# y from high and low parts of x and of the condition's weights, in three fp32r passes from the ninth tile on

## The reference

```python
W = cond_weights[condition]                      # (64, 64, 64)
y = einsum('bct,bcd->bdt', x, W)                 # (64, 64, 1024)
base = einsum('bsi,oi->bso', y, W_org)
q = einsum('bi,ki->bk', y.mean(axis=1), Wq)
coeffs = softmax(einsum('bk,ek->be', q, lora_keys) / sqrt(128))
h = einsum('bsi,eir->bser', y, lora_down)        # 8 experts, rank 64
delta = einsum('be,bser,ero->bso', coeffs, h, lora_up)
out = x + base + delta
```

## Time and profile before

| | |
|---|---|
| median of 3 runs | 714.96 us (714.73 to 715.47) |
| profiled execution | 714.7 us, span 712.9 us |
| PE busy | 701.1 us (98%) |
| PE weight loads | 587.1 us (82%), beside the matmuls |
| DVE busy | 505.9 us (71%) |
| ACT busy | 286.5 us (40%) |
| POOL busy | 118.2 us (17%) |
| instructions | 10677 |

### The profile page before, as it was taken

How to read it: one execution, slowest core, us unless ns; L and a number is a source line. 1 busy time by engine, 2 the same in 40 slices (tenths; PEclk the granted TensorE clock), 3 DMA queues, 4 the chain that set the end, 5 groups by cost and what they waited for, 6 DMA issues and landing times.

```text
span 712.9 us, 10677 instructions
## 1 busy us (share of the span) xinstructions
PE 701.1 (98%) x3345; PEld 587.1 (82%) x3345; DVE 505.9 (71%) x821; ACT 286.5 (40%) x580; POOL 118.2 (17%) x108
## 2 busy tenths in 40 slices
PE   8999999999999999999999999999999999999997
PEld 7877787888888888888888878888888888888876
DVE  3888687585784864655656997786777677776774
ACT  4456665856666742443524822221122222211220
POOL 2210000000000000000000033323332333333360
PEclk9999999999999999999999999999999999999999
DMA  8987376484684754423443846666676776766732
GB/s 240 280 260 232 106 231 209 145 255 149 192 244 149 207 194 128 137 104 90 135 160 121 316 136 194 221 214 219 219 235 237 236 236 220 233 203 213 268 119 88
DMA packets 100986, 138.60 MB, mean 194 GB/s; under 512 B 18874, under 2 KB 70082, under 8 KB 98114
## 3 DMA queue, kind: packets, MB, share of 16 engines
q1 hardware_dynamic: 100592, 137.85, 60.0%
q10 hardware_dynamic: 338, 0.07, 0.0%
HBM read 82.32 MB, written 55.57 MB: 193 GB/s over the span
## 4 chain that ended last, share of the span: by engine, by line
PE 87%; DVE 6%; issue 4%; DMA 1%; SPq 1%; ACT 1%; POOL 0%; DVEq 0%; ACTq 0%; POOLq 0%
PE x_ps L1456 23%; PE w_ps L1456 17%; PE x_ps L1378 11%; PE h_ps L1378 11%; PE x_ps L1412 11%; PE w_ps L1412 8%; PE y_ps L1337 6%; DVE tb_l L873 1%; DVE tu_l L873 1%; DVE blk L876 1%; DMA t_dram<-st 1%; DVE up_raw L873 1%; DVE ysum L889 1%; DMA cw_sb<-in_L_cond_weights_dram 0%; DVE ba_l L873 0%
## 5 line engine op out<-in xcount | busy, mean ns | idle before, releaser
L566 POOL TENSOR_TENSOR blk<-blk,blkx 128x512 f32<-128x512 f32 x60 | 93.1, 1552 | 276.3 <-DMA blkx<-in_x_dram 160.4
L876 DVE TENSOR_TENSOR blk<-w_ps,blk 128x512 f32<-128x512 f32 x96 | 66.1, 688 | 68.1 <-PE w_ps L1412 32.4
L1456 PE MATMUL x_ps<-tb_h,ba_h 128*128 128x512 f32 x256 | 100.0, 390 | 0.8 <-DVE ba_l L873 0.4
L1456 PE MATMUL x_ps<-tb_l,ba_h 128*128 128x512 f32 x256 | 99.6, 389 | 0.0
L1456 PE MATMUL x_ps<-tb_h,ba_l 128*128 128x512 f32 x256 | 99.6, 389 | 0.0
L602 ACT ACTIVATE ba_h<-bs 128x512 fp32r<-128x512 f32 x64 | 38.1, 626 | 125.7 <-DVE bs L873 125.7
L1456 PE MATMUL w_ps<-tb_h,ba_h 128*128 128x512 f32 x192 | 74.9, 390 | 0.0
L1456 PE MATMUL w_ps<-tb_h,ba_l 128*128 128x512 f32 x192 | 74.7, 389 | 0.0
L1456 PE MATMUL w_ps<-tb_l,ba_h 128*128 128x512 f32 x192 | 74.7, 389 | 0.0
L602 ACT ACTIVATE ba_h<-yb 128x512 fp32r<-128x512 f32 x48 | 28.4, 621 | 101.9 <-DMA yb<-y_dram 101.9
L876 DVE TENSOR_TENSOR blk<-x_ps,blk 128x512 f32<-128x512 f32 x64 | 42.5, 683 | 34.2 <-PE x_ps L1456 34.2
(11 more groups left out here) (100 smaller groups left out, 1407.8 us busy)
## 6 DMA issues: line engine op xcount, KB each, us to landing
x_sb<-in_x_dram SPq DMA_DIRECT2D x32, 512.0 KB, 4.3
y_dram<-y_full SPq DMA_DIRECT2D x64, 256.0 KB, 3.1
yb<-y_dram SPq DMA_DIRECT2D x32, 512.0 KB, 7.3
out_dram<-blk SPq DMA_DIRECT2D x64, 256.0 KB, 3.9
blkx<-in_x_dram SPq DMA_DIRECT2D x30, 512.0 KB, 6.8
r_dram<-blk SPq DMA_DIRECT2D x56, 256.0 KB, 2.5
blk<-r_dram SPq DMA_DIRECT2D x14, 1024.0 KB, 6.7
t_dram<-st SPq DMA_DIRECT2D x16, 448.0 KB, 4.3
```

The source lines that it names most:

```text
L566: pool.tensor_tensor(blk[p % 3][:, b, :], blk[p % 3][:, b, :], blkx[:, h, n, :], ALU.add).then_inc(x_added, 1)
L876: nc.vector.tensor_tensor(dst, a, b, ALU.add).then_inc(done, 1)
L1456: mm = nc.tensor.matmul(bank, ba[s][n][:, k, :], tb[w][n][:, k, :], start=(first and k == 0 and i == 0), stop=(k == 3 and i == 2), skip_gr ...
```

## The change

From tile 8 on (TS = 8), y is made of parts. The two buffers of x for tile t are: raw and then, in place, the low part in buffer t % 2; the high part in buffer 2 + t % 2, both as `x_hl`, an fp32r view of the same memory as `x_sb`. So there are two buffers of raw x in place of four, and `load_x(t)` waits for the tile two back. ACT's `split_x(t)` copies x to its high part (128x1024, fp32r), DVE's subtracts it. POOL makes two instructions of each tile's weights: the high part `cwh` (in the memory of cws) and the low part `cwl`. PE makes three matmuls of 128 columns per product: high x high, high x low, low x high.

Each loop q splits the third and fourth tile of its own y (4q+6, 4q+7) amid the h blocks, in loops 1 to 6, and the first two of the next loop's (4q+8, 4q+9) amid the up products, in loops 0 to 5. To make room, `yg` moves into the memory of `gs`, with waits in `gate_sums` for whoever reads gs; two semaphores are folded into others.

```diff
@@ -90,6 +90,8 @@
         yq = [at(f"yq_{s}", 90112 + 16384 * n, [P, KC, N], F32R) for n, s in enumerate("hl")]
         y_full = at("y_full", 122880, [P, 8, 4, P])
         x_sb = at("x_sb", 139264, [P, 4, IN])
+        x_hl = at("x_hl", 139264, [P, 4, IN], F32R)
         g32 = at("g32", 155648, [P, 2, EC, 2 * P])
         ga = [at(f"ga_{s}", 163840 + 7168 * n, [P, NS, 2, P], F32R) for n, s in enumerate("hl")]
         gs = at("gs", 178176, [P, 4, 2, P])
...
@@ -131,13 +133,17 @@
         cw_sb = small("cw_sb", [P, 4, BT, C])
         cws = small("cws", [P, 3, BT, 2, C // 2])
+        cwh = at("cwh", spot[0] - 12 * P, [P, 3, BT, 2, C // 2], F32R)
+        cwl = small("cwl", [P, 3, BT, 2, C // 2], F32R)
         ident = small("ident", [P, P])
         ones_r = small("ones_r", [P, P], F32R)
         gate = small("gate", [P, E, KC])
         keys_sb = small("keys_sb", [E, K])
         keys_t = small("keys_t", [K, E])
         ysum = small("ysum", [P, KC, BQ])
-        yg = small("yg", [P, BQ, E, KC])
+        yg = at("yg", 178176, [P, BQ, E, KC])
         z = small("z", [P, BQ * E])
         zs = small("zs", [P, 2, BQ * E], F32R)
         ssb = small("ssb", [P, BQ, E])
...
@@ -284,6 +291,24 @@
         def tile_made(t):
             return max(made(2 * t), made(2 * t + 1))
+        TS = 8
+        def x_at(t):
+            return t % 4 if t < TS else t % 2
+        def x_count(t):
+            return 16 * (t // 4 + 1 if t < TS else 2 + (t - 6) // 2)
+        def cw_count(t):
+            return t + 1 if t < TS else TS + 2 * (t - TS + 1)
+        def x_high(t):
+            return x_hl[:, 2 + t % 2, :]
+        def x_low(t):
+            return x_hl[:, t % 2, :]
         def copied(n):
             if n >= 8:
                 return y_copied, n - 3
...
@@ -316,16 +341,16 @@
         @block.sync
         def _(sp):
             def load_x(t):
-                i = t % 4
+                i = x_at(t)
                 if t >= 4:
-                    sp.wait_ge(y_done, tile_made(t - 4))
+                    sp.wait_ge(y_done, tile_made(t - 4 if t < TS + 2 else t - 2))
                 sp.dma_start(x_sb[:, i, :], x_v[t, :, :]).then_inc(x_loaded[i], 16)
             def load_cw(t, batches=range(BT)):
                 i = t % 4
                 if t >= 4:
-                    sp.wait_ge(cw_ready, t - 3)
+                    sp.wait_ge(cw_ready, cw_count(t - 4))
                 for b in batches:
                     which = sp.value_load(cond_sb[0:1, BT * t + b:BT * t + b + 1], min_val=0, max_val=NCOND - 1)
                     sp.dma_start(cw_sb[b * C:(b + 1) * C, i, b, :], cond_w[which, :, :]).then_inc(cw_loaded[i], 16)
...
@@ -455,8 +480,11 @@
                 for m in range(4):
                     store_y(n + 2 * m)
                     store_y(n + 2 * m + 1)
+                    if q == 0 and m < 2:
+                        load_x(t + 4 + m)
+                    elif q > 0 and t + 2 + m < T:
+                        load_x(t + 2 + m)
                     if q < NQ - 2:
-                        load_x(t + 4 + m)
                         load_cw(t + 4 + m)
                     if 1 <= q <= 4 and m == 1:
                         if q < 4:
...
@@ -548,8 +576,14 @@
                 pool.wait_ge(cw_loaded[i], 16 * BT * (t // 4 + 1))
                 if t >= 3:
                     pool.wait_ge(y_done, tile_made(t - 3))
-                pool.tensor_copy(cws[:, t % 3, :, :, :],
-                                 cw_sb[:, i, :, :].rearrange("p b (d h) -> p b h d", h=2)).then_inc(cw_ready, 1)
+                turned = cw_sb[:, i, :, :].rearrange("p b (d h) -> p b h d", h=2)
+                if t < TS:
+                    pool.tensor_copy(cws[:, t % 3, :, :, :], turned).then_inc(cw_ready, 1)
+                    return
+                high = cwh[:, t % 3, :, :, :]
+                pool.tensor_copy(high, turned).then_inc(cw_ready, 1)
+                pool.wait_ge(cw_ready, cw_count(t) - 1)
+                pool.tensor_tensor(cwl[:, t % 3, :, :, :], turned, high, ALU.subtract).then_inc(cw_ready, 1)
             def add_xz(b):
...
@@ -631,6 +665,11 @@
                     act.wait_ge(*((h_part, n // 8) if r == 0 else (h_done, EC * (n // 8))))
                 copy(yq[0][:, 4 * r:4 * r + 4, i * P:(i + 1) * P], y_full[:, n % 8, :, :], y_hi[r])
+            def split_x(t):
+                act.wait_ge(x_loaded[x_at(t)], x_count(t))
+                act.wait_ge(y_done, tile_made(t - 2))
+                copy(x_high(t), x_sb[:, t % 2, :], x_hi)
             def split_down(n):
                 act.wait_ge(down_loaded[n], 16)
                 copy(down_piece(0, n), raw_piece(n), down_hi)
...
@@ -809,6 +852,8 @@
                 take_r(j0, 2, P6, r2_ready)
                 hi_sum(j1, P6, 1)
                 take_r(j1, 0, P1, r1_ready)
+                if q < NQ - 2:
+                    split_x(4 * q + 8)
                 hi_block(j1, P2, 0, 1)
                 if q == 0:
                     split_y(n)
...
@@ -825,6 +870,8 @@
                 else:
                     split_t(P6, slice(0, 2))
                 take_r(j0, 1, P3, c12_ready)
+                if q < NQ - 2:
+                    split_x(4 * q + 9)
                 hi_sum(j1, P3, 3)
                 if more:
                     split_y(n + 1)
...
@@ -899,6 +946,11 @@
                 sub(yq[1][:, 4 * r:4 * r + 4, i * P:(i + 1) * P], y_full[:, n % 8, :, :],
                     yq[0][:, 4 * r:4 * r + 4, i * P:(i + 1) * P], y_lo[r])
+            def split_x(t):
+                dve.wait_ge(x_hi, t - TS + 1)
+                sub(x_low(t), x_sb[:, t % 2, :], x_high(t), x_lo)
             def split_down(n):
                 dve.wait_ge(down_loaded[n], 16)
                 dve.wait_ge(down_hi, n + 3)
...
@@ -914,6 +966,12 @@
             def gate_sums(q):
                 dve.wait_ge(y_summed, 8 * q + 8)
+                if q >= 1:
+                    for n in (P5, P6):
+                        dve.wait_ge(ga_hi[n], 2 * q)
+                        dve.wait_ge(ga_lo[n], 2 * q)
+                    dve.wait_ge(s_ready[3], 2 * q)
                 nc.vector.tensor_tensor(yg[:, :, :, :],
                                         ysum[:, :, :].rearrange("p k b -> p b k").unsqueeze(2).to_broadcast([P, BQ, E, KC]),
                                         gate[:, :, :].unsqueeze(1).to_broadcast([P, BQ, E, KC]),
...
@@ -1211,6 +1270,7 @@
                     dve.wait_ge(tu_sum, 2)
                     sub(U22, U22, U11, tu_sum)
                 elif more:
+                    split_x(4 * q + 7)
                     sum_y(n + 4)
                     sum_y(n + 5)
                 else:
...
@@ -1325,18 +1389,31 @@
         def _(pe):
             def make_y(n):
                 t, r = n // 2, n % 2
-                i = t % 4
-                pe.wait_ge(x_loaded[i], 16 * (t // 4 + 1))
-                pe.wait_ge(cw_ready, t + 1)
+                pe.wait_ge(x_loaded[x_at(t)], x_count(t))
+                pe.wait_ge(cw_ready, cw_count(t))
+                if t >= TS:
+                    pe.wait_ge(x_hi, t - TS + 1)
+                    pe.wait_ge(x_lo, t - TS + 1)
                 if n in BEFORE:
                     pe.wait_ge(*copied(BEFORE[n]))
                 elif n >= 10:
                     pe.wait_ge(*copied(n - 2))
                 for k in range(4):
                     col = (4 * r + k) * P
-                    mm = nc.tensor.matmul(y_bank(n)[:, k * P:(k + 1) * P], x_sb[:, i, col:col + P],
-                                          cws[:, t % 3, :, :, :].rearrange("p b h d -> p (b h d)"),
-                                          start=True, stop=True)
+                    out = y_bank(n)[:, k * P:(k + 1) * P]
+                    if t < TS:
+                        mm = nc.tensor.matmul(out, x_sb[:, t % 4, col:col + P],
+                                              cws[:, t % 3, :, :, :].rearrange("p b h d -> p (b h d)"),
+                                              start=True, stop=True)
+                    else:
+                        high = cwh[:, t % 3, :, :, :].rearrange("p b h d -> p (b h d)")
+                        low = cwl[:, t % 3, :, :, :].rearrange("p b h d -> p (b h d)")
+                        nc.tensor.matmul(out, x_high(t)[:, col:col + P], high, start=True, stop=False,
+                                         skip_group_check=True)
+                        nc.tensor.matmul(out, x_high(t)[:, col:col + P], low, start=False, stop=False,
+                                         skip_group_check=True)
+                        mm = nc.tensor.matmul(out, x_low(t)[:, col:col + P], high, start=False, stop=True,
+                                              skip_group_check=True)
                 mm.then_inc(y_done, 1)
             def make_h(q, a, r):
```

More of the change, by code:

```diff
@@ L168, in adaln_ffn @@
         wq_loaded = sem("wq_loaded")
-        zero_ready = sem("zero_ready")
         up_loaded = [sem(f"up_loaded_{n}") for n in range(EC)]
@@ L184, in adaln_ffn @@
```

(15 more changed lines are left out.)

## The result

The changed kernel takes 740.67 us (740.32 to 741.26, four runs), the kernel before 714.85 us: a ratio of 1.036, 95% interval 1.034 to 1.038. The forecast was 739.0 us. The profiled execution took 740.32 us with a span of 738.5.

The account below looks back on a forecast made before the run. PE bounds the kernel, y by its weight loads. From 714.7 us: +21.4 for the third pass, +1.0 and +2.8 for up-stage stalls, -0.9 for a stall that goes, sum 739.0 us; range 732 to 746 us.

Parts of the forecast that it names:

- The load as the bound: y's matmuls, tiles 8 to 31: loading 128x128 weights sets the pace, 0.1116 us each, so the third pass adds 21.4 us.
- The quicker stream: y's matmuls: 128 fp32r columns stream in 0.06 us against 0.107 or so; the saving hides under the loads, gives nothing.
- Rivals A and B: y's fp32r loads hide wholly (A: 710.2 or 715 us, chance 0.09) or in part (B: 721 us, chance 0.05).
- Rival D: y's products: narrow fp32r matmuls stream at a quarter of the rate, +80 us, 795 us; chance 0.02.
- Cost: nothing: Splits of x's third and fourth tiles amid the h blocks: PE does not wait for them, no time added.
- the cover: x's third tile of a loop: two longer y tiles ahead of it give its low part 0.9 us of cover.
- The up stages' terms: Splits of x amid the up products delay DVE's add: +2.8 us in q=0, +0.2 us in each of q=1 to 5.
- The stall that goes: Loop q=1: PE's 1.5 us wait for a low part of y shrinks behind longer y, -0.9 us.
- Rival C: DVE late by a whole subtraction in each up stage and at x's third tile each loop: 12 us more, 751; chance 0.06.

## Why the prediction was right

**The load as the bound.** This was the step on which the sign hung, and it held: 0.1115 us from load to load against 0.1116 in the sum. Its evidence was indirect, a pace that was alike for 8 and 128 columns and an fp32r load after idle time as long as a float32 one. The runs with half the weights, half the columns and 256 columns show it directly. The term came out 0.8 us larger than in the sum, since a tile grew by 0.927 and not 0.893 us. A whole pass more or less costs 0.893 exactly; the other 0.03 us lies in the step from float32 to fp32r, at the tile's edges: two passes, with as many loads as before, take 1.74 us a tile against 1.70.

**The quicker stream.** The 0.06 us of the earlier trace rows was real, and worth nothing, as the sum had it. Rivals A and B go with it: no steady row of 128x128 fp32r loads was quicker than 0.11 us. Rival D falls by the same rows. The Trainium skill (TensorE: Matmul & The Clock Gate, section on weight-path perf modes) has a fast load for types other than FP32; no run here shows it for fp32r weights. The same page of the Trainium skill (section on the back-to-back issue gap) has 81 ns a pair at 128 columns; here it is 111.

**The splits.** "Cost: nothing" for those amid the h blocks was right but for q=1: 0.4 us. The prediction read the cover from loop q=3 and took it for every loop, while in q=1 the low part is ready 1.9 us later. I take DVE's six late sums, which hold up the loop's first steps, for the origin of that; no run tests it. That the longer tiles give the cover is shown by the run with two passes, where about 1.1 us a loop came back in q=2 to 4. The up stages' terms held, +3.1 for 2.8 and 0.2 each, and moving the splits shows that it was their place ahead of end_c22(j1).

**The stall that goes.** -1.0 for -0.9; the row of waits of the kernel after, against 1.5 in the earlier trace rows:

```profile
PE x_ps L1455 <- DVE yq_l L920: 0.6, 1, 0.6
```

What I hadn't foreseen is the -0.4 in q=1's up stage. Before, its 19.72 us held 0.6 more than the 19.14 of the later loops. The timelines of ACT and PE, kernel before:

```profile
109.03 0.60 ACT L602 ACTIVATE blk<-x_ps 128x512 f32<-128x512 f32 x1 [1.37 <-DMA t_dram<-st]
...
109.68 0.50 PE L1412 MATMUL x_ps<-tu_h,ga_h 128*128 128x512 f32 x1 [0.24 <-ACT blk L602]
```

PE waited for ACT's copy, which had waited 1.37 us for a transfer. In the kernel after ACT's copy at this place waits for no transfer, only 0.46 us for PE. That the later start took the wait away is likely, not tested.

Rival C didn't come about: in the up stages DVE was late by 0.2 us and not by a whole subtraction, and amid the h blocks PE's longer tiles let DVE keep up.

**The size.** The forecast of 739.0 is 1.7 us under the median, 1.3 under the profiled execution. Terms too small (0.8 for the tiles, 0.3 in q=0, 0.4 for x's third tile, and the 0.6 of the base products, which had no term) were in part made up by q=1's up stage, 0.6 us under its term. That the sum came as close as this owes something to that; the sign and 22.2 of the 25.8 us don't, since they are the third load.

## What to carry to other kernels

Ask of a narrow matmul what it loads before asking what it streams: with 128x128 of four-byte weights, here 0.11 us a load, anything under some 256 fp32r columns moved is paid for by the load, and three passes cost three loads. Splitting an operand for rounded passes doesn't pay where each load moves 128 columns; whether it does at the 512 columns of the other products no run here compares. And look for what would be next: here DVE's results came so close ahead of PE's need that a y of half the length gained 5.5 us of 20.6.

## What the runs showed of the hardware

- A float32 and an fp32r weight load of 128x128 take the same 0.11 us; with 64 columns it is 0.06 us or less. The number of moved columns (8, 64, 128) doesn't change the pace. Two loads with 128 and 256 fp32r columns take 0.23 us together, against 0.22 with 128 each.
- PE's clock could fall to 1.2 GHz, at some 1.65 us a fall: behind 0.57 us of idling in one run, behind 1.46 to 2.45 us in others, and once with no idling to be seen. It also held through 2.12, 2.35 and 2.44 us, and behind 3.4 us it fell in one execution and held in another with the same matmuls. The changed kernel itself showed no fall in its profiled execution.
